# Inverse transform of the convolution spectrum: 64 slots stacked on 128 rows, and the four other slots of four graphs in one split product

## The reference

```python
# layer 0: agg = eps*x + A@x ; silu(rmsnorm(agg@W1 + b1)) @ W2 + b2
# layer 1: a convolution branch, a message branch, and a gated unit over both
h = relu(bn(conv1d(xc, conv1_w, 0)))
h = bn(conv1d(h, conv2_w, 8))              # 17 taps over the 128 nodes
x_conv = relu(h + xc)
A = exp(-dist(x @ w_se.T)) * adj ; x_nmp = A @ relu(x @ w_msg.T + b_msg)
gi = concat(x_conv, x_nmp) @ w_ih.T + b_ih ; gh = x @ w_hh.T + b_hh
out = (1 - z) * tanh(gi_n + r * gh_n) + z * x
# layer 2: three propagation steps with adj / row sums, leaky relu
# layer 3: two-layer MLP on eps*x + adj@x
```

## Time and profile before

| | |
|---|---|
| time, median of three runs | 1186.98 us (1185.79 to 1189.19) |
| profiled execution | 1185.8 us, of which the span of the trace is 1183.8 us |
| PE (matmul) busy | 1129.8 us, 95% |
| DVE busy | 867.6 us, 73% |
| ACT busy | 736.1 us, 62% |
| POOL busy | 593.3 us, 50% |
| DMA engines | 21.7% of the span, 82.58 MB |
| mean granted TensorE clock | 0.984 of full |

### The profile page before, as it was taken

How to read it: one execution, slowest core, us unless ns; L and a number is a source line. 1 busy time by engine, 2 the same in 40 slices (tenths; PEclk the granted TensorE clock), 3 DMA queues, 4 the chain that set the end, 5 groups by cost and what they waited for, 6 DMA issues and landing times. The chain is left out here.

```text
span 1183.8 us, 24192 instructions
## 1 busy us (share of the span) xinstructions
PE 1129.8 (95%) x7851; PEld 1026.6 (87%) x7851; DVE 867.6 (73%) x2564; ACT 736.1 (62%) x1328; POOL 593.3 (50%) x528
## 2 busy tenths in 40 slices
PE   7899999999999879799999999999999999999984
PEld 7799999999999769678889899898989898989874
DVE  3378877777777713126878888888888888888984
ACT  3444455555555432156677778787878777787765
POOL 1044443434343226424565757575666666675754
PEclk9999999999999999979999999999999999999988
DMA  4123322232322134511011212121212121120001
GB/s 154 54 72 98 100 90 90 90 94 95 98 90 64 54 120 163 169 39 55 30 54 37 73 38 73 37 74 38 73 38 64 47 58 53 41 69 29 10 18 45
DMA packets 46962, 82.58 MB, mean 70 GB/s; under 512 B 5172, under 2 KB 15224, under 8 KB 46584
## 3 DMA queue, kind: packets, MB, share of 16 engines
q1 hardware_dynamic: 46840, 81.05, 21.7%
HBM read 55.34 MB, written 25.69 MB: 68 GB/s over the span
## 5 line engine op out<-in xcount | busy, mean ns | idle before, releaser
L162 POOL TENSOR_TENSOR rstd<-ve,minus_half 128x4 f32<-128x4 f32 x128 | 153.5, 1200 | 150.0 <-DVE ve L1012 144.3
L162 POOL TENSOR_TENSOR r_rms<-ms,minus_half 128x4 f32<-128x4 f32 x32 | 32.3, 1010 | 236.5 <-DVE ms L976 236.5
L454 PE MATMUL bank<-w,s 128*128 128x128 f32 x1024 | 135.1, 275 | 0.4 <-DVE y L990 0.4
L454 PEld LDWEIGHTS bank<-w,s 128*128 128x128 f32 x1024 | 126.9, 192 | 3.5 <-issue 0.5
L1322 POOL TENSOR_TENSOR edge_adj<-edge,atc 128x512 f32<-128x512 f32 x32 | 40.8, 1275 | 101.8 <-ACT edge L828 101.8
L755 ACT ACTIVATE s<-hn,cols 128x512 f32<-128x512 f32 x128 | 84.9, 712 | 10.9 <-DVE hn L983 10.3
L983 DVE SCALAR_TENSOR_TENSOR hn<-bank,cols,rv 128x512 f32<-128x512 f32 x128 | 86.8, 737 | 1.0 <-ACT rv L159 0.6
L149 PE MATMUL bank<-agg_hi,w_hi 128*128 128x512 f32 x192 | 86.9, 452 | 0.0
L1002 DVE BATCH_NORM_STATS2 stats<-y 128x6 f32<-128x128 f32 x384 | 82.7, 277 | 2.6 <-POOL y L1354 2.5
L155 PE MATMUL bank<-at,x_rows 128*128 128x128 f32 x512 | 71.3, 284 | 9.6 <-ACT x_rows L902 6.0
L155 PEld LDWEIGHTS bank<-at,x_rows 128*128 128x128 f32 x512 | 67.1, 199 | 14.1 <-ACT x_rows L902 7.3
(11 more groups left out here) (192 smaller groups left out, 3450.4 us busy)
## 6 DMA issues: line engine op xcount, KB each, us to landing
at<-in_at SPq DMA_DIRECT2D x32, 256.0 KB, 3.0
x_rows<-in_x SPq DMA_DIRECT2D x32, 256.0 KB, 2.9
ad<-in_ad SPq DMA_DIRECT2D x32, 256.0 KB, 2.7
x_scratch<-x SPq DMA_DIRECT2D x32, 256.0 KB, 3.2
x1c<-x_scratch SPq DMA_DIRECT2D x32, 256.0 KB, 2.6
atc<-in_at SPq DMA_DIRECT2D x32, 256.0 KB, 2.9
yh<-yh_scratch SPq DMA_DIRECT2D x32, 256.0 KB
out<-out_rows SPq DMA_DIRECT2D x32, 256.0 KB, 4.1
```

The costliest lines, as they stand in the source:

```text
L162: return nc.gpsimd.tensor_tensor(to[:], base[:], minus_half[:], ALU.pow)
L454: last = pe.matmul(bank[7][:, g, :], s[c][:, g, :], w2[:, c, :], start=(c == 0 and g == 0), stop=(c == H0 - 1), skip_group_check=True)
```

## The change

It does four things.

1. The first 64 slots are stored as before, but `load_yh` puts the cosine halves on rows 0 to 63 and the sine halves on rows 64 to 127 of one tile, so that `inverse` does four fp32 products of 128 x 128 x 128 in place of eight of 68 rows. For this the graphs are numbered g*32+k in `xh` and in the DRAM scratch, in place of 4k+g, and a load reads pieces of 512 B.
2. The last four slots of the four graphs of a group (4 graphs x 2 halves x 4 slots = 32 rows) are stored apart, 16 small DMAs. They are loaded into `rest_full` four times over (rows 32r), eight parts of four groups with four DMAs each; ACT makes the high part over all 128 rows (`rest_high`), DVE overwrites the quarters 1 and 3 with the low part (`rest_low`, two instructions of 32 rows x 512). With a block-diagonal constant, also split, one fp32r product of 128 rows x 512 gives hi*hi + lo*hi + hi*lo (+ lo*lo) for all four graphs. Parts 0 and 1 are made in part two, at pairs 18, 19, 22 and 23; parts 2 to 7 in part three, at the very start of ACT's and DVE's turns 1 to 6. The loads come from SP at its pair 14, and at the start of its turns 0 to 5.
3. The last four slots are computed first in part two, the negations follow that order, and the ring `spectrum` uses other tiles. One more constant (256 KB) is loaded and split.
4. `row_sums` and `load_ad` move eight turns later in part one, so that the last one falls into the last turn, 42, which was empty. Some waits are written out that an earlier one on the same engine already covers, the semaphores `z_gate_x` and `z_gate_n` are renamed, and `TURNS3` is 40 in place of 41 (the last turn was empty).

```diff
 PE, part two and three
+        SLOT_ORDER = list(range(MAIN, SLOTS)) + list(range(MAIN))      # MAIN = 64
-                slot_product(psum[:, 0:2 * P], 2 * p)
-                slot_product(psum[:, 2 * P:4 * P], 2 * p + 1).then_inc(sem["slot_ps"], 1)
+                slot_product(psum[:, 0:2 * P], SLOT_ORDER[2 * p])
+                slot_product(psum[:, 2 * P:4 * P], SLOT_ORDER[2 * p + 1]).then_inc(sem["slot_ps"], 1)
             def inverse(k):
                 landed(pe, yh_in, k, 32)
-                free(pe, ("pts_l0 pts", k))
+                pe.wait_ge(sem["rest_hi"], k // PART + 1)
+                pe.wait_ge(sem["rest_lo"], 2 * (k // PART + 1))
+                free(pe, ("pts_l0 pts", k), ("msg", k), ("c2_res", k - 1))
+                pe.matmul(flat(bank[6]), rest[:, k, :], rest_idft[:], start=True, stop=False, skip_group_check=True)
                 for g in range(G):
-                    pe.matmul(bank[6][:, g, :], yh[k % YH_RING][:, g, 0, :], idft[:, 0, :], start=True, stop=False)
-                    last = pe.matmul(bank[6][:, g, :], yh[k % YH_RING][:, g, 1, :], idft[:, 1, :], start=False,
-                                     stop=True)
+                    last = pe.matmul(bank[6][:, g, :], yh[k % YH_RING][:, g, :], idft[:], start=False,
+                                     stop=(g == G - 1), skip_group_check=True)
 SP
-                stage(load_ad, t - 1)
+                stage(load_ad, t + 2 - 11)
-                sp.dma_start(to[0:64], of_group[0:64]).then_inc(yh_in[k % YH_RING], 16)
-                sp.dma_start(to[64:SLOTS], of_group[64:SLOTS]).then_inc(yh_in[k % YH_RING], 16)
+                sp.dma_start(to[0:MAIN], of_group[:, :, 0]).then_inc(yh_in[k % YH_RING], 16)
+                sp.dma_start(to[MAIN:P], of_group[:, :, 1]).then_inc(yh_in[k % YH_RING], 16)
+                    for g in range(G):
+                        for s in range(2):
+                            sp.dma_start(rest_dram[g, :, slot - MAIN + s].rearrange("h k o -> k h o"),
+                                         of_pair[GROUPS * g:GROUPS * (g + 1), s]).then_inc(rest_stored[p], 16)
+            def load_rest(i):
+                if i >= 2:
+                    sp.wait_ge(sem["rest_lo"], 2 * (i - 1))
+                else:
+                    sp.wait_ge(set_dve, DVE_LATE - 1)
+                for r in range(P // (G * REST)):
+                    sp.dma_start(rest_full[i % 2][G * REST * r:G * REST * (r + 1)],
+                                 rest_dram.rearrange("g h s k o -> (g h s) k o")[:, PART * i:PART * (i + 1)]
+                                 ).then_inc(rest_in[i % 2], 16)
             for t in range(TURNS3):
+                if t + 2 < PARTS:
+                    load_rest(t + 2)
                 stage(load_x1, t + 2)
 ACT
-                copy(xh[:, :, first:first + 2], psum).then_inc(sem[("xh0", "xh1")[half]], 1)
+                to = xh[:].rearrange("p c (g k) -> p c g k", g=G)[:, :, 2 * half:2 * half + 2, k]
+                copy(to, psum).then_inc(sem[("xh0", "xh1")[half]], 1)
+            def rest_high(i):
+                act.wait_ge(rest_in[i % 2], 16 * 4 * (i // 2 + 1))
+                copy(rest[:, PART * i:PART * (i + 1), :], rest_full[i % 2]).then_inc(sem["rest_hi"], 1)
             for t in range(TURNS3):
+                if 2 <= t + 1 < PARTS:
+                    rest_high(t + 1)
                 stage(x1_high, t)
 DVE
-                stage(row_sums, t - 3)
+                stage(row_sums, t - 11)
+            def rest_low(i):
+                dve.wait_ge(sem["rest_hi"], i + 1)
+                for r in (1, 3):
+                    own = slice(G * REST * r, G * REST * (r + 1))
+                    low = rest[own, PART * i:PART * (i + 1), :]
+                    V.tensor_tensor(low, rest_full[i % 2][own], low.bitcast(F32), ALU.subtract
+                                    ).then_inc(sem["rest_lo"], 1)
             for t in range(TURNS3):
+                if 2 <= t + 1 < PARTS:
+                    rest_low(t + 1)
                 stage(gate_u, t - 2)
                 stage(gate_v, t - 2)
 POOL
-                Q.tensor_scalar(neg_b[:, slot % G, :], wh[:, 2 * slot + 1, :], -1.0, None, ALU.mult
+                slot = NEGATED[i]
+                Q.tensor_scalar(neg_b[:, i % G, :], wh[:, 2 * slot + 1, :], -1.0, None, ALU.mult
```

More of the change, by code:

```diff
@@ L192, in graph_layers @@
         hcp, hc = rows("hcp"), rows("hc")
-        y0 = rows("y0")
-        s = [rows(f"s{c}") for c in range(H0)]
+        last_s, last_hn = rows("last_s"), rows("last_hn")
         stage_tile = [rows(f"stage{i}") for i in range(3)]
@@ L197, in graph_layers @@
         wh = sb("wh", [P, HALVES, P])
+        y0 = rows("y0")
+        s = [rows(f"s{c}") for c in range(H0 - 1)] + [last_s]
+        hn = [rows(f"hn{c}") for c in range(H0 - 1)] + [last_hn]
         w1f = flat(stage_tile[0])
@@ L223, in graph_layers @@
         pick = sb("pick", [64, P], F32R)
-        idft = sb("idft", [SLOTS, 2, P])
+        idft = sb("idft", [P, P])
+        rest_idft_full, rest_idft = sb("rest_idft_full", [P, G * P]), sb("rest_idft", [P, G * P], F32R)
+        rest_full = [wt_full[:, PART * i:PART * (i + 1), :] for i in range(2)]
+        rest = sb("rest", [P, GROUPS, P], F32R)
         eps3_ident = sb("eps3_ident", [P, P])
@@ L228, in graph_layers @@
         row_inv = sb("row_inv", [P, B])
-        x1c = [rows(f"x1c{i}") for i in range(X1C_RING)]
-        atc = [rows(f"atc{i}") for i in range(ATC_RING)]
+        x1c = [rows(f"x1c{i}") for i in range(2)]
+        atc = [rows(f"atc{i}") for i in range(2)]
         pts_l, pts_r = rows("pts_l"), rows("pts_r")
-        yh = [sb(f"yh{i}", [SLOTS, G, 2, P]) for i in range(YH_RING)]
+        yh = [rows(f"yh{i}") for i in range(YH_RING)]
         x1_hi, x1_lo = ([rows(f"x1_{n}{i}", F32R) for i in range(2)] for n in ("hi", "lo"))
+        x1c += [rows(f"x1c{i}") for i in range(2, X1C_RING)]
+        atc += [rows(f"atc{i}") for i in range(2, ATC_RING)]
         edge, edge_adj, msg = rows("edge"), rows("edge_adj"), rows("msg")
@@ L288, in everything_second @@
             engine.wait_ge(sem["neg_b"], SLOTS - 1)
-            for p in range(PAIRS - STORES, PAIRS):
-                landed(engine, yh_stored, p)
+            for p in list(range(REST_PAIRS)) + list(range(PAIRS - STORES, PAIRS)):
+                stored_pair(engine, p)
         @block.sync
@@ L382, in _ @@
                 store_slots(p)
+                if p == 14:
+                    for i in range(REST_PAIRS):
+                        stored_pair(sp, i)
+                    load_rest(0)
+                    load_rest(1)
             for p in range(PAIRS - STORES, PAIRS):
-                landed(sp, yh_stored, p)
+                stored_pair(sp, p)
             everything_second(sp)
@@ L1426, in layouts @@
     share = np.where(slot == 0, 1.0, 2.0) / L
+    inverse = waves(node).transpose(1, 2, 0) * share[:, None, None]
+    rest_idft = np.zeros((4, G, REST, G, P), np.float32)
+    for g in range(G):
+        rest_idft[:, g, :, g, :] = inverse[MAIN:].transpose(1, 0, 2).reshape(REST, P)
+    rest_idft = rest_idft.reshape(P, G * P)
     return {
```

135 lines of the change are left out of this document (82 added, 53 removed).

## The result

The changed kernel takes 1196.6 us (median of 6 runs, 1191.28 to 1202.85), the kernel before 1186.72 (6 runs, 1185.79 to 1190.89). The ratio is 1.007, 95% interval 1.0048 to 1.0092: some 10 us slower, where I had forecast 10 faster. The profiled execution took 1191.66 us, its span 1189.9, which is among the shortest of its runs; against the 1185.8 and 1183.8 of before that is 5.9 and 6.1 us more. The runs of the changed kernel scatter over 12 us, those of before over 5, and that turns out to be part of the answer.

The account below looks back on a forecast made before the run. PE was taken to bound parts two and three. The terms +0.2 - 1.0 + 8.3 - 16.9 = -9.4 gave 1176.4 us from the profiled 1185.8, or 1177.6 from the median; forecast 1177, range 1165 to 1190.

Parts of the forecast that it names:

- The inverse itself: Part three, each group: inverse costs 1.05 us in place of 1.70, lone product at 0.24, saving 0.65.
- Rival B: Part three: the inverse's lone product costs 0.52 us, so the kernel takes 1185 us; chance 0.12.
- The later turns: Part three, turns 7 to 32: each of 26 turns 0.65 us shorter, 16.9 saved, with 0.26 left before messages.
- rival C: Later turns: the chain z gate, out_rows, `c_res` becomes the bound and no gain remains there, 1194.5 us; chance 0.08.
- Turns 2 to 6: Part three: DVE's `rest_low` waits for ACT's `rest_high`, delaying hop1 and messages; +8.3 us, five shorter inverses included.
- my bound: Part three, turns 2 to 6: from 3.3 us gained to 13 lost if DVE's whole delay counts.
- Edit (d): Part one, copy into `xh` with larger stride: nothing, or at most some 0.4 us in each of twelve turns, 5 us.
- Part two and its covers: Part two: 16 small stores, queued loads and the split of parts 0 and 1 cost nothing; uncovered stores 2 to 5 us.
- edit (f): Part two: the first slot now needs a negation, +0.2 us.
- Edit (c): Later row sums: the last ends at about 435.4 us, the first negations and copies don't hang on it; costs nothing.
- Turn 1: Part three, first turn at the low clock: the shorter inverse saves 1.0 us.
- The range: Whole kernel's time: from 1165 to 1190 us.

Follow-up runs that it names:

- e4_pick128: The kernel before, with the lone product of messages on 128 rows in place of 64; 1173.52 us, ratio 0.9881.
- e5_best: e3_both with the lone product of messages on 128 rows in place of 64 as well; 1157.44 us, ratio 0.9735.
- e1_contig: The changed kernel with the old numbering of the graphs (4k+g), so ACT's copy writes adjacent pairs again; 1184.42 us, ratio 0.9969.
- e6_strided: The kernel before with only the new graph numbering (g*32+k), so ACT's copy writes with the larger stride; 1194.26 us, ratio 1.0064.
- e3_both: The changed kernel with the old graph numbering and the last slots' preparation moved into idle gaps of turns 1 to 6; 1167.38 us, ratio 0.9827.
- e8_high_only: The changed kernel with `rest_high` moved to ACT's gap of the turn before, `rest_low` left at the head of DVE's turn; 1178.37 us, ratio 0.992.
- e7_early_sums: e5_best with `row_sums` and `load_ad` back in their old turns of part one; 1157.23 us, ratio 0.9736.

## Why the prediction was wrong, by its own steps

**The inverse itself: right.** 1.05 in place of 1.70, the lone product at 0.24, as read from the trio of the earlier trace rows. e4_pick128 shows why the row that spoke against it was no evidence: its 0.52 belongs to the 64 rows, not to standing alone. Rival B falls with it.

**The later turns: right.** 0.647 a turn against 0.65, and no new bound: the weight load of messages starts 0.25 us behind the end of `c_res`, where I had seen 0.26 left. The chain of rival C was near all the same: in e5_best, with a turn 0.33 shorter, messages waits for `c_res` in every turn. The measured 1196.6 lies close to rival C's 1194.5, but not by its mechanism. From turn 8 on the gain is 15.51 + 1.66 = 17.2, forecast 15.6 for 24 turns and nothing for the end.

**Turns 2 to 6: the mechanism right, the size wrong.** Waits before hop1 and before messages, put down to `w3h` and `c_res`, stood in the profile as foretold, but the term measured +16.0 from turn 2 to turn 8 where I had +6.5. For turns 3 to 6 alone that is 17.3 in place of 7.8, above even the 13 of my bound. PE's idle time of 14.0 us is not far above what my +8.3 implied, 8.3 + 5 x 0.65 = 11.6. (For turn 5 my rows give 2.1, not the 2.2 that I wrote; nothing hangs on it.) Two things are missing from the term. First, a step that is late meets other work: `u` fell on POOL's `edge_adj` in turns 2 and 3 (1.64 in place of 0.69), and `v` was some 4.5 us late in turn 3 (2.50 + 1.40 + 0.95, less the 0.40 that `u` had waited in the earlier trace rows) rather than the 3.3 that I had. The Trainium skill (SBUF — State Buffer, Who interferes with whom) says that a DVE instruction with two inputs in SBUF contends with a GpSimd one that reads SBUF; the trace agrees, and I had set such a doubling only as a bound for `rest_low`. Second, and larger, the clock. From `c_res` of group 1 to that of group 7, the lengthening of 16.0 is made of 12.1 more idle time (the six waits in it, the first only from 534.38 on), less 6 x 0.65 = 3.9 of shorter inverses, plus about 8 that is neither: PE working at the lower clock. The windows bear that out: ten-microsecond stretches with a granted clock of 0.83, 0.83, 0.83, 0.92 and 0.74 lack 8.5 us of full speed. In e1_contig the same reckoning gives 13.6 = 12.1 - 3.9 + 5.4, and the clock columns there lack 5.1: the same waits, a smaller price, since the clock stayed up after one of them. My sum treated a wait as worth its own length. I had even written down, from the earlier trace rows, that the clock was low at the seam and that "PE had idled between the parts", and did not carry that over to the waits that I was adding myself. The Trainium skill (TensorE: Matmul & The Clock Gate, HAM oscillation) describes a kernel in which waits for DMA between bursts of products send the clock to half rate again and again, and in which the slow stretch costs half its length. The waits here are for other engines; the trace agrees on the price, with products of a trio at 0.43 us in place of 0.23 behind the first wait.

**Edit (d), the stride in `xh`: wrong, the term mis-sized.** I said nothing or 5 us; it is 0.25 us in each of 22 turns (5.6 us from group 9 to group 31), and 6.5 by the medians of e6_strided, so also outside its bound. Two errors stand behind it. I gave a cost only to the last twelve turns, because I took PE as the bound of part one from its busy share; but PE waited for this very copy in every turn from group 9 on, which the weight loads show and the busy share does not. And I had no row for a stride and leaned to nothing. Here the Trainium skill had a rule that I passed over (SBUF — State Buffer, Door 1: The DMA port swizzle): SBUF works in lines of 16 bytes and wants two accesses to a line for full speed. The old copy wrote pairs of neighbouring 4-byte values, the new one single values, the nearest 128 bytes apart. By that rule the new form is slower than the old, and the trace agrees: 652 ns in place of 400.

**Part two and its covers: right.** In the profiles where the clock was not low at its start, part two is 0.2 us longer than before with all the stores and the split in it (59.58 in e1_contig, e3_both and e8_high_only, 59.37 before and in e6_strided). That is the size that I had for the negation of the first slot, edit (f), though no run separates it from the new order of the slots. The 16 stores, the loads in SP's queue, and the split at pairs 18 to 23 are hidden. (An issue takes 0.51 us by my row, three in 1.53, not 0.4; the cover held all the same.) Edit (c) costs nothing (e7_early_sums). The +2.27 of the changed kernel's own profile is the clock again, 0.89 in its first 20 us.

**Turn 1**, with turns 0 and 2 around it: -1.41, where I had -1.0 + 0.5 = -0.5. That it came out near is luck, two misses that offset each other. In e3_both, without the wait at the head of the turn, this stretch takes 30.02 us in place of 34.30, 4.3 less, so the wait costs 2.9 us here and not 0.5, and the rest brings 4.3 and not 1.0. Most of that is the clock's, 0.77 in this stretch of e3_both and 0.70 before. How much of it the shorter inverse brought is open, since e6_strided, with the old inverse, has 0.75 there.

**The range.** Of the 15.5 us between -9.4 and +6.1, 5.0 come from part one up to its last `agg_hi`, 9.5 from turns 3 to 8, 3.4 from the stretch behind it and part two (beyond the 0.2 that I had), and 2.5 go the other way. The median is another 4 us above the profile: the runs of one kernel differ by how long the low clock lasts. In e6_strided, 1191.1 us go with a mean clock of 0.985 and 1203.6 with 0.971. I had no case for that; a change that adds idle time to PE, in a kernel whose runs already differ by the clock, has its tail on the slow side.

**What stays open.** Between the last `agg_hi` and the first product of part two the same work takes 50.0 us (before, e3_both, e4_pick128), 52.7 (e5_best) or 56.4 (e8_high_only). PE is idle for 12.7 to 13.0 us of that stretch in every kernel, a quarter of it, and the longer ones show a clock below 1.00 in parts of it (down to 0.50 from 420 to 430 us in e8_high_only), the shorter ones 1.00 all through. The versions with the strided copy are all among the longer ones (51.3 to 56.4), but e1_contig, e5_best and e7_early_sums, without it, are too (52.6, 52.7 and 53.4). As the idle time is nearly the same in all, its amount does not decide whether the clock falls. What does was not settled, and no kernel was run that fills this stretch with work for PE.

## What to carry to other kernels

Small work added to two engines at the head of a turn is cheap or dear by its place: here, from turn 2 to turn 8, the same preparation cost 20 us at the head of the turn and 2 behind its rush, because a step that waits for another engine holds up everything queued behind it. Price each wait that you add to PE at more than its length, since the lower clock after it cost two thirds as much again here, and 0.45 as much in e1_contig, and look for a place where nothing due soon stands behind the wait. And an engine that is busy for all of a stretch can still wait in every turn: read the start of its weight loads against the end of the copy that frees the bank. A distance that is small and the same in every turn is the mark of a wait.

## What the runs showed of the hardware

- A copy of 128 x 272 fp32 values from PSUM to SBUF on ACT takes 400 ns when it writes pairs of neighbours, and 652 ns when it writes single values, the nearest 128 bytes apart.
- One fp32r product of 64 rows between products of 128 costs 0.39 us more than one of 128 rows: about 0.1 of it is in the four fp32 products behind it, the rest around the product itself.
- After waits of PE of 1.80 (with one of 0.78 just ahead), 3.62, 2.29 and 3.06 us in turns that were otherwise full, the granted clock was at its lower level for a few microseconds; after 1.75 us (at 571.68), and after the waits of some 0.5 us in e3_both, it was not. In e1_contig it was not after one of 3.07 us either, so the length of the wait alone does not decide.
- A step of PE that was released by a copy of ACT or a step of DVE had its weight load start 0.11 to 0.12 us after the end of that step, in every turn.
- A DVE operation with two inputs in SBUF, 128x512, took 1.64 us in place of 0.69 while POOL combined two tiles of the same size.
